# Cross-attention: which of three shifted-score units stand in front of the first gap

## The reference

```python
q = (x @ Wq).reshape(B, N, HEADS, hd).transpose(0, 2, 1, 3)        # 16 heads of 32
k = (context @ Wk).reshape(B, M, HEADS, hd).transpose(0, 2, 1, 3)  # 750 keys
v = (context @ Wv).reshape(B, M, HEADS, hd).transpose(0, 2, 1, 3)
scores = jnp.einsum('bhid,bhjd->bhij', q, k) * scale
scores = jnp.where(context_mask[:, None, None, :], scores, max_neg)
attn = jax.nn.softmax(scores, axis=-1)
out = jnp.einsum('bhij,bhjd->bhid', attn, v)
return out.transpose(0, 2, 1, 3).reshape(B, N, DIM) @ Wo
```

## Time and profile before

| | |
|---|---|
| median of three runs | 3951.14 us |
| lowest, highest | 3950.44, 3954.77 us |
| the profiled execution, its own time | 3952.49 us |
| its span | 3950.7 us |
| mean granted TensorE clock | 0.97 of full |
| busy: TensorE, VectorE, ScalarE, GpSimd | 93%, 61%, 45%, 33% |

### The profile page before, as it was taken

How to read it: one execution, slowest core, us unless ns; L and a number is a source line. 1 busy time by engine, 2 the same in 40 slices (tenths; PEclk the granted TensorE clock), 3 DMA queues, 4 the chain that set the end, 5 groups by cost and what they waited for, 6 DMA issues and landing times. The chain is left out here.

```text
span 3950.7 us, 84965 instructions
## 1 busy us (share of the span) xinstructions
PE 3683.9 (93%) x28086; PEld 3168.4 (80%) x28086; DVE 2402.1 (61%) x5621; ACT 1763.3 (45%) x4321; POOL 1303.4 (33%) x1200
## 2 busy tenths in 40 slices
PE   7999999999769999999999999749999999999997
PEld 6888888888557887877788887549889898898986
DVE  6788888888646767666766766465333333333332
ACT  4554545455335555555555555312333333333332
POOL 1333333333225555555555555310202102012011
PEclk9999999999879999999999999769999999999998
DMA  4222222222233334343433343212323333243231
GB/s 121 58 57 58 56 61 63 53 62 52 76 109 97 102 104 108 102 117 92 107 100 104 106 105 95 60 53 86 108 85 109 106 88 113 73 120 109 80 102 54
DMA packets 315627, 347.04 MB, mean 88 GB/s; under 512 B 45263, under 2 KB 232247, under 8 KB 315540
## 3 DMA queue, kind: packets, MB, share of 16 engines
q1 hardware_dynamic: 305940, 318.31, 29.5%
q0 software_dynamic: 9600, 27.58, 2.4%
HBM read 181.68 MB, written 38.65 MB: 56 GB/s over the span
## 5 line engine op out<-in xcount | busy, mean ns | idle before, releaser
L1518 DVE TENSOR_REDUCE x_mx<-x_psS 112x1 f32<-112x752 f32 x512 | 479.2, 936 | 422.7 <-PE x_psS L1093 417.5
L2236 DVE TENSOR_TENSOR hid<-e_psU,act_g 128x280 f32<-128x280 f32 x256 | 115.1, 449 | 735.0 <-PE e_psU L34 735.0
L1350 ACT ACTIVATE x_pt<-x_psE 125x448 f32<-125x448 f32 x768 | 389.4, 542 | 274.5 <-PE x_psE L1105 268.6
L989 POOL TENSOR_TENSOR part<-x_pt 125x448 f32<-125x448 f32 x256 | 293.0, 1145 | 636.9 <-ACT x_pt L1350 636.4
L1875 POOL TENSOR_TENSOR ex_y<-ex_y,ex_cur 112x2560 f32<-112x2560 f32 x8 | 45.5, 5686 | 1014.7 <-ACT ex_y L2066 1014.7
L548 POOL TENSOR_TENSOR qks<-qks,cos 128x448 f32<-128x448 f32 x128 | 148.0, 1156 | 678.0 <-DMA qks<-qk 678.0
L2019 ACT ACTIVATE act_g<-e_psG 128x280 f32<-128x280 f32 x256 | 103.8, 405 | 509.1 <-PE e_psG L34 509.0
L1093 PE MATMUL x_psS<-k_st,q_st 97*112 97x376 f32 x1024 | 290.9, 365 | 38.9 <-DVE x_mx L1518 25.7
L32 PE MATMUL e_psG<-ex_hi,g_hi 128*128 128x280 f32 x1024 | 300.7, 294 | 8.1 <-DVE g_lo L2089 6.7
L32 PE MATMUL pj<-xT_hi,win_hi 128*128 128x224 f32 x1024 | 302.6, 296 | 1.4 <-DVE xT_lo L584 1.3
L991 POOL TENSOR_TENSOR part<-part,x_pt 125x448 f32<-125x448 f32 x256 | 292.9, 1144 | 20.1
(11 more groups left out here) (280 smaller groups left out, 10808.0 us busy)
## 6 DMA issues: line engine op xcount, KB each, us to landing
k_st<-kT SPq DMA_DIRECT2D x768, 93.8 KB, 2.1
raw_g<-in_L_ffn_wg SPq DMA_DIRECT2D x128, 256.0 KB, 3.1
raw_u<-in_L_ffn_wu SPq DMA_DIRECT2D x128, 256.0 KB, 3.4
raw_d<-in_L_ffn_wd SPq DMA_DIRECT2D x128, 256.0 KB, 2.7
qks<-qk SPq DMA_DIRECT2D x512, 56.0 KB, 2.0
q_st<-qT SPq DMA_DIRECT2D x384, 56.0 KB, 2.0
ctxt<-in_ctx SPq DMA_DIRECT2D x16, 1125.0 KB
xt<-in_x SPq DMA_DIRECT2D x16, 448.0 KB, 3.6
```

Source lines behind the costliest of these rows:

```text
L989: pool.tensor_tensor(part[:], pt[j][:, 0, :], pt[j][:, 1, :], ALU.add).then_inc(parted, 1)
L1350: act.activation(pt[j][:, i, :], psE[(j + i) % 2][0:KR, 0:2 * T], ACT.Exp, scale=XD ** -0.5).then_inc(exp_done, 1)
L1518: dve.tensor_reduce(mx[:, j, h:h + 1], psS[0:HT, :, 0:376], AX.XY, ALU.max).then_inc(s_taken, 1)
L2236: dve.tensor_tensor(h[i][:, halves[s]], psU[:, 0:CH], act_g[i][:, halves[s]], ALU.mult).then_inc(S["mul"], 1)
```

## The change

In every sub-step the second unit of shifted scores moves from in front of the first gap to behind it, and on ScalarE its exponential moves likewise. The first gap itself, the second gap, the number of instructions, the banks and all semaphores stay. VectorE's and GpSimd's lists stay. Where the first gap is empty (sub-steps 0 to 2 of the last group of the last batch) and in the tail, the order is the same in both kernels.

```diff
@@ -1231,10 +1231,10 @@
                                         done(U(f"M0_{gp}") if g else unit_of(b - 1, "M0_3"))
                                     elif j == 2:
                                         done(U(f"M1_{g}"))
-                                    shifted(n - 1, gp, j, (0, 1))
+                                    shifted(n - 1, gp, j, (0,))
                                 first_gap(g, j)
                                 if prev:
-                                    shifted(n - 1, gp, j, (2,))
+                                    shifted(n - 1, gp, j, (1, 2))
                                 scores(n, g, j, 1)
                                 second_gap(g, j)
                             if prev:
@@ -1452,10 +1452,10 @@
                             n, prev = t + g, not (first and g == 0)
                             for j in range(4):
                                 if prev:
-                                    exps(n - 1, j, (0, 1))
+                                    exps(n - 1, j, (0,))
                                 first_gap(g, j)
                                 if prev:
-                                    exps(n - 1, j, (2,))
+                                    exps(n - 1, j, (1, 2))
                                 second_gap(g, j)
```

## The result

The changed kernel took 3960.0 us (median of 20 runs, 3955.84 to 3964.61) against 3953.4 us for the kernel before in the same number of runs: ratio 1.0016, 95% interval 1.0009 to 1.0023. That is 6.6 us slower, with 3.6 to 9.1 us as the interval; forecast were 6.3 us and no change in the sense of a 0.2% bound. The absolute time is 2.6 us above the forecast of 3957.4 and 1.0 us above the upper bound of 3959.0. Of the 2.6 us, 2.3 come from the kernel before, which measured 3951.14 in its first three runs and 3953.4 over twenty, and 0.3 from the cost of the change. Against the 3953.4 the bound of 7.9 us holds.

What follows compares the result with a forecast made beforehand. TensorE, busy 93%, was taken as the bound, so only its waits counted. Two spots, 14 times 0.225 us each, gave 6.3 us: 3958.8 profiled, 3957.4 as median of runs; range 3947 to 3963, no-change bounds 3943.2 to 3959.0.

Steps and rivals of the forecast that it cites:

- TensorE's own time: Reordered shifted scores on TensorE: no gap between matmul kinds added, banks alternate as before; cost 0.
- the first gap's earliness: First-gap product on TensorE ready 0.21 us sooner, its bank already free; gain 0, upper end 15 us.
- Part 2: The step on the first-gap product coming 0.21 us sooner: gain 0, upper end 15 us.
- The slip: ScalarE's third exponential 0.225 us later in sub-steps 0 to 2, GpSimd's sum following; bounds 0 to 0.44.
- Spot A: Group 0, sub-steps 0 and 1: later GpSimd addition holds VectorE's norm, delaying TensorE's scores; 0.225 us, 14 times.
- h1 of sub-step 1: Group 0's second-half scores on TensorE: held about 0.15 us, swallowed by the later wait before sub-step 2's scores.
- Spot B: Group 3, sub-step 2: L1557 ends later behind GpSimd, delaying sub-step 3's second-half scores; 0.225 us, 14 times.
- the period: Time of one batch, read from L1557's starts: 87.6 us forecast instead of 87.2.
- The wait behind the maximum: TensorE's scores waiting for VectorE's row maximum, 1300 to 2450 us: up from 20.3 us by about 6.
- Rival A: Group 0, sub-step 1: L1570 gets in ahead of GpSimd's addition; 5.7 us faster in all, 3945.5 us; chance 0.10.
- Rival B: No delay of the third exponential reaches TensorE: 3951.1 us, batch time unchanged; chance 0.15.
- rival C: Values block waits longer behind ScalarE in sub-step 3: 3 to 6.6 us more, say 3962 us; chance 0.13.

## Why the prediction was right

*TensorE's own time 0, the first gap's earliness 0.* Right: thirteen sub-steps in the new order gave 1.0001. The groups without norm steps kept their lengths but for 0.03 us: from values block to values block 22.67 and 26.00 us before, 22.70 and 26.00 after. The 0.03 (0.4 us in all) is not shown to be the order's: the kernel in the old order with three empty instructions, which was no slower than the kernel before, has 22.70 as well. Part 2 is borne out where it could have been wrong: VectorE's wait for the copy of the maxima fell from 13.3 to 3.9 us in the stretch, and TensorE gained nothing by it: the groups without norm steps got no shorter.

*The slip, 0.225 us.* By the rounded rows 0.44 less 0.21 is 0.23. Measured 0.208 on L1557 (382 to 590 ns). The bound of 0.44 that was kept for the range turned out to be what ScalarE's order alone does.

*Spot A, 0.225.* Group 0 went from 20.15 to 20.36 us, 0.21. That h1 of sub-step 1 would be held for about 0.15 on the way was seen as 0.15. *Spot B, 0.225.* Group 3 went from 18.35 to 18.58, 0.23; the bracket from 0.19 to 0.41. Together 0.44 a batch, 6.2 us in fourteen, the change's own part as the traces show it; with the 0.03 above it is the period's 0.47, 6.6 us. That this equals the measured 6.6 to the tenth is luck, with an interval of 3.6 to 9.1.

*What would show it.* L1557 at 0.6: 0.59. L1570's longest still 1.1: 1.121. The period 87.6: 87.63. The wait behind the maximum was to grow by about 6 us and grew by 2.8 in the stretch: that is spot B's 0.22, thirteen times. Spot A's growth went mostly to h1 of sub-step 1, held for 0.15 us behind overlapping matmul records, where no bracket shows it. The indicator was badly chosen, the step it stood for held.

*Rival A* was priced wrongly: it forgot L1573, the next norm step. With one sub-step's slip of 0.22 us the hold goes over to it and nothing is gained; it takes 0.44 us. The same oversight cost the expectation for sub-step 0 alone, where L1568 was the one that came to stand in GpSimd's way. In the change itself both sub-steps slip alike, so the order in which VectorE and GpSimd arrive was kept, as the argument against rival A had it. That was also the reason why the change cost 6.6 us and not 23. The margin was thin: 0.04 us between the addition and L1570 before, 0.05 after. The prediction saw what a larger slip in sub-step 1 might bring, and put 5.7 us on it; it did not list the other side, VectorE late against GpSimd by one slip, which costs 23.3 us (sub-step 0 alone) and lies far outside its range.

*Rival B* is excluded by the period and *rival C* by the values block's wait, unchanged at 0.75 us a time.

## What to carry to other kernels

An instruction that ends earlier or later on an idle engine matters where a third engine's start hangs on it and that engine holds a fourth. In this kernel the chain was exponential, GpSimd addition, VectorE norm step, row maximum, scores. So before an idle engine's slack is booked as cover, look for short operations with several durations, 160, 999 and 1129 ns here: the longer ones end where another engine's instruction ends. Keep such small steps away from GpSimd's work, or at a place where nobody waits; here that was worth three times what the order of the matmuls cost. And when two queues meet within 0.05 us, follow every later instruction of the chain, not the one that is caught today.

## What the runs showed of the hardware

The Trainium skill, "SBUF — State Buffer", section "SBUF: two separate sides", states that the first to start keeps the shared pair for its whole instruction and the other blocks. The runs agree as far as VectorE is the one that waits: arriving 0.05 us behind the addition made a step of 0.16 us take 1.12 (L1576 in the run with sub-step 1 alone), arriving 0.2 us ahead of it cost nothing beyond the 0.16 us of the step itself (L1573 at 1652.55 with sub-step 1's exponentials moved), and in the lines shown a held step ends within 0.02 us of the end of the addition. That VectorE can hold GpSimd in the same way, no run here shows.

A 112x2 operation on VectorE can so take longer than the maximum over 112x752 scores beside it, 0.94 us: its length was 0.16 us free and up to 1.13 held.

A pause of TensorE of 1.57 us in an otherwise full stretch was followed by the lower clock in six of fourteen batches, at 1.55 us each; pauses of 0.79 us at the same place never were, in thirteen batches (granted clock 1.00 over 1300 to 2450 us). Why in these six and not in the others is open.

Three empty GpSimd instructions between a wait and an addition delayed it by nothing that the trace shows; an addition of eight numbers took 0.19 us and delayed it by 0.16.
